# Softmax division moved behind P·V, a quarter of the transposed copies on VectorE, and a Newton root for the layer norm

## The reference

```python
# layer 0: attention with 16 heads of 32, no dependence between graphs
q = split_heads(x @ Wq.T); k = split_heads(x @ Wk.T); v = split_heads(x @ Wv.T)
bias = (adj + adj)[:, None]
a = einsum('bhnd,bhmd->bhnm', q, k) * D**-0.5 + bias
a = where(any(a != 0, axis=-1, keepdims=True), a, -inf)
p = where(isnan(softmax(a)), 0, softmax(a))
o = einsum('bhnm,bhmd->bhnd', p, v)           # -> (b, n, 512)
x = layernorm(x + o @ Wo.T)                   # (x - mean) / sqrt(var + 1e-5)
# layer 1: one of four experts per graph, batch norm over the graphs of an expert
top1 = argmax(x.mean(axis=1) @ router_w + router_b)
out = adj @ (x @ expert_w[top1])
y = relu(batchnorm_of_the_expert(out) * gamma[top1] + beta[top1])
x = layernorm(x + y)
```

## Time and profile before

| | us |
|---|---|
| median of three runs | 2745.92 |
| lowest, highest run | 2745.65, 2753.64 |
| span of the profiled execution | 2748.4 |
| of it: before the first unit's transposes | 0 to 89 |
| graph 0 | 89 to 239 |
| graphs 1 to 14, about 152 each | 239 to 2355 |
| graph 15 | 2355 to 2497 |
| tail of layer 1 | 2497 to 2580 |
| batch norm and last phase | 2580 to 2748 |

### The profile page before, as it was taken

The page is one execution under the profiler, slowest core; times in us unless marked ns, Lnnn a source line. Parts: engine busy times, 40 slices in busy tenths (PEclk is TensorE's granted clock), DMA queues, the critical chain, the costliest instruction groups (busy, mean ns, idle before and its releaser), DMA issues.

```text
span 2748.4 us, 57103 instructions
## 1 busy us (share of the span) xinstructions
PE 2333.9 (85%) x14976; PEld 1816.4 (66%) x14976; DVE 2121.6 (77%) x5107; ACT 1722.6 (63%) x3838; POOL 1771.9 (64%) x3148
## 2 busy tenths in 40 slices
PE   2778999989899898989998998989899998986533
PEld 2556777767677676767676776767677776765432
DVE  2687878788887878788887878787888878773488
ACT  0566776667666666667676666667677666763232
POOL 0777776768777777768676777767687777771000
PEclk7789998999999999999999999999999999988765
DMA  6676564645555564646455554646455555533497
GB/s 212 197 223 214 155 204 143 208 127 172 154 183 158 168 182 151 197 144 197 137 173 154 175 167 149 196 142 210 133 161 164 177 155 176 159 92 120 170 327 255
DMA packets 215956, 479.61 MB, mean 175 GB/s; under 512 B 41424, under 2 KB 49616, under 8 KB 208720
## 3 DMA queue, kind: packets, MB, share of 16 engines
q1 hardware_dynamic: 215632, 475.71, 55.1%
HBM read 274.23 MB, written 67.11 MB: 124 GB/s over the span
## 4 chain that ended last, share of the span: by engine, by line
PE 61%; DVE 17%; issue 9%; POOL 4%; ACT 3%; SPq 3%; DMA 2%; DVEq 1%; ACTq 0%; POOLq 0%
PE t_bank L334 12%; PE p_bank L252 11%; PE p_bank L253 10%; PE p_bank L254 10%; PE o_bank L347 8%; PE s_bank L325 6%; DVE att L494 3%; DVE att L468 3%; SPq L646 2%; POOL fold L617 2%; PE p_bank L288 2%; DVE ln_raw L1004 2%; POOL fold L619 1%; PE p_bank L293 1%; ACT att L407 1%
## 5 line engine op out<-in xcount | busy, mean ns | idle before, releaser
L617 POOL TENSOR_TENSOR fold<-att 128x256 f32<-128x256 f32 x1024 | 809.8, 791 | 538.7 <-DVE nmax L468 440.4
L446 ACT ACTIVATE pt<-t_bank 128x512 f32<-128x512 f32 x1024 | 610.5, 596 | 583.1 <-PE t_bank L334 571.4
L468 DVE CUSTOM_DVE_ANT_0 att<-s_bank,adj_t 128x512 f32<-128x512 f32 x1024 | 699.6, 683 | 333.9 <-PE s_bank L325 323.1
L407 ACT ACTIVATE att<-att,nmax 128x512 f32<-128x512 f32 x1024 | 737.3, 720 | 128.2 <-POOL fold L617 98.4
L494 DVE TENSOR_SCALAR att<-att,small 128x512 f32<-128x512 f32 x1024 | 739.9, 723 | 9.3
L334 PE MATMUL t_bank<-ident,att 128*128 128x128 f32 x4096 | 645.5, 282 | 46.6 <-issue 40.7
L334 PEld LDWEIGHTS t_bank<-ident,att 128*128 128x128 f32 x4096 | 515.2, 145 | 229.2 <-issue 101.8
L325 PE MATMUL s_bank<-k_stack,q_stack 128*128 128x512 f32 x1024 | 507.5, 496 | 108.0 <-DVE nmax L468 106.9
L619 POOL TENSOR_TENSOR fold<-fold 128x128 f32<-128x128 f32 x1024 | 528.2, 516 | 80.3
L624 POOL TENSOR_TENSOR fold<-fold 128x64 f32<-128x64 f32 x1024 | 351.7, 343 | 98.1 <-POOL fold L619 22.9
L347 PE MATMUL o_bank<-pt,v 128*32 128x256 f32 x4096 | 276.6, 415 | 31.9 <-ACT pt L446 15.1
(11 more groups left out here) (150 smaller groups left out, 3554.6 us busy)
## 6 DMA issues: line engine op xcount, KB each, us to landing
q_stack<-qk_t SPq DMA_DIRECT2D x1024, 64.0 KB, 2.0
k_stack<-qk_t SPq DMA_DIRECT2D x1024, 64.0 KB, 2.0
qk_w<-qk_split SPq DMA_DIRECT2D x123, 512.0 KB, 4.1
slot_a<-vo_split SPq DMA_DIRECT2D x16, 2048.0 KB, 8.0
slot_b<-vo_split SPq DMA_DIRECT2D x16, 2048.0 KB, 9.9
slot_a<-expert_split SPq DMA_DIRECT2D x16, 2048.0 KB, 7.9
stage<-in_xT SPq DMA_DIRECT2D x16, 1024.0 KB, 14.0
adj_t<-in_adj SPq DMA_DIRECT2D x64, 256.0 KB, 3.0
```

Of the source, the lines that this page charges most:

```text
L407: eng.activation(att[:, u % 4, j, :], att[:, u % 4, j, :], ACT.Exp, bias=nmax[:, u % 4, j:j + 1], scale=-1.0, accum_out=rsum[:, u % 4, j:j ...
L446: eng.activation(pt[:, j, :, (u % 2) * P:(u % 2 + 1) * P], t_bank[r % 2][:, :].rearrange("p (m n) -> p m n", m=NT), ACT.Copy).then_inc(act ...
L468: eng.tensor_tensor_reduce(out=att[:, u % 4, j, :], in0=s_bank[r % 2][:, :], in1=adj_t[:, t, :], scale=-2.0, scalar=3.0e38, op0=ALU.add, o ...
L617: eng.tensor_tensor(fold1[:, :], a[:, 0:256], a[:, 256:512], ALU.add).then_inc(pool_fold1, 1)
```

## The change

The scaling of att goes. Transposes now wait for exp alone, and ACT copies heads 0 to 2 into pt while DVE copies head 3 (DVE_TURNED, dve_turned, dve_pt). Once per pair DVE forms weight = live / rsum, 128 x 8 numbers (dve_weights, in step 3 of the pair's first unit). In pe_pv eight fp32 matmuls with the weight, broadcast to 32 columns, as stationary side and the identity as moving side write these numbers as rows into the free half of the same o_bank; P·V itself is moved from the end of the pair's second slot behind the scores of the next slot's first step, in front of that step's transposes. When the bank is emptied, ACT copies the broadcast half to spread (act_spread_out), DVE multiplies it with the product (dve_scale), and the high and low parts of ot are taken from spread. EMPTIED is later by a unit for pairs 4 to 6.

The root of the layer norm of layer 0 is computed on DVE by 13 dependent instructions on 128 x 4 numbers (dve_rstd, in (6, 2)): a first guess from the bits and three Newton steps. The square root on ACT and the reciprocal go. The statistics of M- are aggregated at once (bn_stats, bn_aggr, and one copy per graph), and the batch norm's sums take four instructions fewer. The last phase's root stays on ACT.

```diff
-NORM_UNITS = 2
+TOTAL_UNITS = 2
+DVE_TURNED = 3
...
-        EMPTIED = {0: -1, 5: 0, 7: 1, 8: 2, 9: 3, 10: 4, 12: 5, 14: 6}
+        EMPTIED = {0: -1, 5: 0, 7: 1, 8: 2, 9: 3, 11: 4, 13: 5, 15: 6}
...
+        def wait_turned(eng, b, r):
+            u, j = divmod(r, HG)
+            if j == DVE_TURNED:
+                wait(eng, dve_pt, b, UNITS, u + 1)
+            else:
+                wait(eng, act_pt, b, (HG - 1) * UNITS, (HG - 1) * u + j + 1 - (j > DVE_TURNED))
...
         def pe_turn(eng, b, r):
-            wait(eng, dve_norm, b, STEPS, r + 1)
-            wait(eng, act_pt, b, STEPS, r - 1)
+            wait(eng, act_exp, b, STEPS, r + 1)
+            wait_turned(eng, b, r - 2)
...
-        def pe_pv(eng, b, u):
-            pair, g = u // 2, u // NT
-            wait(eng, act_pt, b, STEPS, 4 * u + 4)
-            wait(eng, dve_ot, b, PAIRS, pair - 1)
-            wait(eng, act_v, b, NT, NT)
+        def pe_pv(eng, b, pair):
+            g, bank = (pair % PAIRS) // 2, o_bank[pair % 2]
+            wait(eng, dve_scaled, b, PAIRS, pair - 1)
+            wait(eng, dve_weight, b, PAIRS, pair + 1)
+            for half in range(2):
+                for j in range(HG):
+                    eng.matmul(bank[j * HD:(j + 1) * HD, (2 + half) * P:(3 + half) * P],
+                               weight[:, pair % 2, half, j:j + 1].to_broadcast([P, HD]), ident[:, :],
+                               start=True, stop=True, tile_position=(0, j * HD))
+            wait(eng, act_pt, b, (HG - 1) * UNITS, (HG - 1) * 2 * (pair + 1))
+            wait(eng, dve_pt, b, UNITS, 2 * (pair + 1))
+            if pair >= 0:
+                wait(eng, act_v, b, NT, NT)
...
+                closes = j == 0 and u >= 0 and u % 2 == 0 and (attends if u else has_prev)
+                turns = attends and r >= 0
+                if turns and not closes:
                     pe_turn(eng, b, r)
                 if (attends and r + LEAD < STEPS) or (has_next and r + LEAD >= STEPS):
                     pe_scores(eng, b, r + LEAD)
+                if closes:
+                    pe_pv(eng, b, u // 2 - 1)
+                if turns and closes:
+                    pe_turn(eng, b, r)
...
-            if attends and u >= 0 and u % 2 == 1:
-                pe_pv(eng, b, u)
...
+        def act_spread_out(eng, b, pair):
+            wait(eng, pe["pv"], b, PAIRS, pair + 1)
+            wait(eng, dve_ot, b, PAIRS, pair)
+            eng.activation(spread[:, :], o_bank[pair % 2][:, 2 * P:4 * P], ACT.Copy).then_inc(act_spread, 1)
...
-                if u == 6 and j == 3 and has_prev:
-                    wait(eng, dve_ln, b, 8, 0)
-                    eng.activation(ln_std[:, :], ln_mv[:, :, 1], ACT.Sqrt, bias=eps_c[:, :]).then_inc(act_std, 1)
...
+        def dve_turned(eng, b, r):
+            u, j = divmod(r, HG)
+            wait(eng, pe["turn"], b, STEPS, r + 1)
+            wait(eng, pe["pv"], b, PAIRS, u // 2)
+            eng.tensor_copy(pt[:, j, :, (u % 2) * P:(u % 2 + 1) * P],
+                            t_bank[r % 2][:, :].rearrange("p (m n) -> p m n", m=NT)).then_inc(dve_pt, 1)
...
-        def dve_normalise(eng, b, r):
-            u, j = divmod(r, HG)
-            eng.tensor_scalar(att[:, u % 4, j, :], att[:, u % 4, j, :], rinv[:, j:j + 1], live[:, j:j + 1],
-                              ALU.mult, ALU.mult).then_inc(dve_norm, 1)
...
+            eng.reciprocal(rinv[:, :, :], rsum[:, at, :]).then_inc(dve_stat, 1)
+            eng.tensor_tensor(weight[:, pair % 2, :, :], rinv[:, :, :], live[:, :, :],
+                              ALU.mult).then_inc(dve_weight, 1)
+        def dve_scale(eng, b, pair):
+            wait(eng, act_spread, b, PAIRS, pair + 1)
+            eng.tensor_tensor(spread[:, :], o_bank[pair % 2][:, 0:256], spread[:, :], ALU.mult).then_inc(dve_scaled, 1)
+        def dve_rstd(eng, b):
+            n = 13
...
+            link(eng.tensor_scalar(ln_var, ln_mv[:, :, 1], EPS, None, ALU.add))
+            link(eng.tensor_scalar(ln_half.bitcast(I32), ln_var.bitcast(I32), 1, None, ALU.logical_shift_right))
+            link(eng.tensor_copy(ln_std, ln_half.bitcast(I32)))
+            link(eng.tensor_scalar(ln_rstd.bitcast(I32), ln_std, -1.0, float(0x5f3759df), ALU.mult, ALU.add))
+            for _ in range(3):
+                link(eng.scalar_tensor_tensor(out=ln_half, in0=ln_var, scalar=-0.5, in1=ln_rstd, op0=ALU.mult,
+                                              op1=ALU.mult))
+                link(eng.tensor_tensor(ln_half, ln_half, ln_rstd, ALU.mult))
+                link(eng.scalar_tensor_tensor(out=ln_rstd, in0=ln_half, scalar=1.5, in1=ln_rstd, op0=ALU.add,
+                                              op1=ALU.mult))
...
+                if attends and r >= 0 and j == DVE_TURNED:
+                    dve_turned(eng, b, r)
...
+                if j == 3 and u >= 0 and u % 2 == 0 and attends:
+                    dve_weights(eng, b, u // 2)
+                if u in EMPTIED and (attends if u else has_prev):
+                    pair = EMPTIED[u]
+                    if j == 1:
+                        dve_scale(eng, b, pair)
...
+                if (u, j) == (6, 2) and has_prev:
+                    dve_rstd(eng, b)
```

More of the change, by code:

```diff
@@ L64, in build_gnn_layers @@
     PAIRS = UNITS // 2
+    BN_OPS = 2 * DT + 1
     HALF_SCALE = 0.5 * float(D) ** -0.5
@@ L114, in build_gnn_layers @@
         rb, iota4 = small[:, 4:8], small[:, 8:12]
-        total, live, rinv = small[:, 12:16], small[:, 16:20], small[:, 20:24]
         ln_std, ln_rstd = small[:, 24:28], small[:, 28:32]
         xmean = small[:, 32:36]
+        ln_var, ln_half = small[:, 12:16], small[:, 16:20]
         rt = small[:, 40:56].rearrange("p (a e) -> p a e", a=4)
@@ L122, in build_gnn_layers @@
         rsum = sb("rsum", [P, 4, HG])
+        total = sb("total", [P, 4, HG])
+        live = sb("live", [P, 2, HG])
+        rinv = sb("rinv", [P, 2, HG])
+        weight = sb("weight", [P, 2, 2, HG])
+        spread = sb("spread", [P, 2 * P])
         ln_raw = sb("ln_raw", [P, NT, 6])
@@ L417, in act_ot_hi @@
                 wait(eng, pe["O"], b, NT, 0)
-            eng.activation(ot[:, 0, g, half * 256:half * 256 + 256], o_bank[pair % 2][:, 0:256],
-                           ACT.Copy).then_inc(act_ot, 1)
+            eng.activation(ot[:, 0, g, half * 256:half * 256 + 256], spread[:, :], ACT.Copy).then_inc(act_ot, 1)
         def act_slot(eng, b, u, kind, kind_before):
@@ L441, in act_slot @@
                 r = HG * u + j
-                if attends and r >= 0:
+                if attends and r >= 0 and j != DVE_TURNED:
                     wait(eng, pe["turn"], b, STEPS, r + 1)
@@ L476, in dve_total @@
-            eng.tensor_reduce(total[:, :], fold2[:, u % 2, :, :], AX.X, ALU.add).then_inc(dve_stat, 1)
-        def dve_live(eng, b, u):
-            wait(eng, dve_norm, b, STEPS, HG * u)
-            wait(eng, dve_logit, b, STEPS, HG * (u + 1))
-            wait(eng, dve_stat, b, 3 * UNITS, 3 * u + 1)
-            eng.scalar_tensor_tensor(out=live[:, :], in0=total[:, :], scalar=0.0, in1=nmax[:, u % 4, :],
-                                     op0=ALU.not_equal, op1=ALU.logical_or).then_inc(dve_stat, 1)
@@ L486, in dve_reciprocal @@
[L486 to L495 removed]
+            eng.tensor_reduce(total[:, u % 4, :], fold2[:, u % 2, :, :], AX.X, ALU.add).then_inc(dve_total_done, 1)
@@ new lines, in dve_weights @@
+        def dve_weights(eng, b, pair):
+            at = slice(2 * pair % 4, 2 * pair % 4 + 2)
+            wait(eng, dve_total_done, b, UNITS, 2 * pair + 2)
+            wait(eng, dve_logit, b, STEPS, 2 * HG * (pair + 1))
+            wait(eng, act_exp, b, STEPS, 2 * HG * (pair + 1))
+            eng.scalar_tensor_tensor(out=live[:, :, :], in0=total[:, at, :], scalar=0.0, in1=nmax[:, at, :],
+                                     op0=ALU.not_equal, op1=ALU.logical_or).then_inc(dve_stat, 1)
+            eng.reciprocal(rinv[:, :, :], rsum[:, at, :]).then_inc(dve_stat, 1)
+            wait(eng, dve_stat, b, 2 * PAIRS, 2 * (pair + 1))
+            wait(eng, pe["pv"], b, PAIRS, pair - 1)
+            eng.tensor_tensor(weight[:, pair % 2, :, :], rinv[:, :, :], live[:, :, :],
+                              ALU.mult).then_inc(dve_weight, 1)
@@ L565, in dve_slot @@
             for j in range(HG):
-                if j == 2 and u in EMPTIED and (attends if u else has_prev):
-                    pair = EMPTIED[u]
-                    g, half = divmod(pair % PAIRS, 2)
-                    wait(eng, act_ot, b, PAIRS, pair + 1)
-                    dve_low(eng, ot[:, 1, g, half * 256:half * 256 + 256], o_bank[pair % 2][:, 0:256],
-                            ot[:, 0, g, half * 256:half * 256 + 256]).then_inc(dve_ot, 1)
                 if u == 6 and has_next:
```

90 lines of the change are left out of this document (44 added, 46 removed).

## The result

The changed kernel takes 2778.55 us (median of 4 runs, 2777.78 to 2779.87) against 2746.18 for the kernel before in the same comparison: ratio 1.0111, 95% interval 1.0097 to 1.0125. It is slower by 1.1%. The forecast was 2769, slower by 0.8%, with 2725 to 2805 as its range. The profiled execution spans 2776.6 us, 28.2 more than before.

A forecast was written before the change was run, and what follows sets the result against it. PE's in-order queue was taken as the bound: 2748.4 + 42 (14 middle iterations at +3.0) - 22 (first) + 1 (last) + 2 (tail) = 2771 us profiled, so 2769 as median; range 2725 to 2805.

The forecast's parts named there:

- Rival 4: Rival on the pair's eight matmuls: weight loads not hidden behind 128 columns, 0.9 us each time, 2813 us; chance 0.15.
- (4,0): Unit 4, step 0, a pair's closing: matmuls +0.48 us, plus +0.2 as P·V waits for DVE's copy of step 3.
- (10,0): Unit 10, step 0, a pair's closing: matmuls paid and P·V waiting for DVE's copy, +0.68 us.
- (2,0): Unit 2, step 0, a pair's closing: score and matmuls replace the 0.7 us wait for V, later score saved, -0.2 us.
- Unit 6: PE's long wait for xt in a middle iteration: removed scalings paid back by the root's 13 instructions, -0.3 us.
- Rival 2: Rival: the root's small instructions overlap, the xt wait opens, middle iterations cost nothing extra, 2729 us; chance 0.17.
- S-0 and the mean: PE's waits in a middle iteration: S-0's low part earlier, -0.6 us; router's mean behind DVE's copy and low part, +0.45.
- (0,0): Unit 0, step 0, a pair's closing in a middle iteration: the eight matmuls paid in full, +0.48 us.
- The first iteration: Graph 0: DVE relieved, POOL's folds next at 1.8 us per step, 128 us, so -22 us.
- the last iteration: Last graph: fewer chunks, second half waits for ACT's copies, a quarter fewer, against the same matmuls: +1 us.
- the tail: From 2497 us on: no attention covers layer norm, mean and router, and the root is longer on DVE: +2 us.
- one of my own signs of being wrong: Listed: middle iteration of 152 us or less, P·V waiting over 1 us for DVE's copy, or first iteration unchanged.

## Why the prediction was right, and where it was not

**The bound.** Right. PE's queue sets the time, and DVE, ACT and POOL lose 620 us of busy time together without any gain. What DVE's work still does is decide when four or five things are ready.

**The eight matmuls.** The price of eight is as forecast at both clocks, 0.46 and 0.85 us against 0.48 and 0.91. Rival 4, 0.9 each, is out: the trace has 0.46 for sixteen loads with 128 columns each. The rule of the Trainium skill that went its way (TensorE: Matmul & The Clock Gate, section "The mechanism"), by which weight loads overlap matmuls in flight only when the row group differs, is not borne out by this trace. My sum of 3.4 us per iteration for all eight pairs, less what they replace, compares with 2.9 that come back without them. That the two are near is in part luck: nothing came back ahead of the P·V of (4,0) and (10,0), where I had them paid. At (2,0) the step holds exactly when iterations of equal clock are compared: 16.66 us from V to P·V before, 16.75 after, forecast +0.1. At (10,0) P·V waits 0.5 for the copy, where I had 0.2.

**Unit 6.** Right by its mechanism: what the change frees is paid back by the root, forecast -0.3, measured +0.1. PE's wait for a logit falls by 2.3 us per iteration and that for xt grows by 2.2. That the 3 us freed come from the scalings is argued, not shown. The root is 3.37 us and not 2.7: one of the thirteen, the shift on integers, takes 0.72 against 0.17 for its neighbours, and without it my 0.21 each is met (twelve in 2.6 us). Rival 2 is right in one half: unit 6 does open, by 3 us, once the thirteen are out, and the kernel is then at 2723, near the 2729 of that rival (2727 if the 2.5 us between profile and median are taken off, as in my other sums). The thirteen do not overlap, so it did not happen.

**S-0 and the mean.** PE's wait for sup fell by 0.6 and that for the mean rose by 0.7, against -0.6 and +0.45. But the wait for x1t rose from 1.0 to 1.3 in the mean, which I had not looked at.

**The loop's turn.** Missed. I counted the matmuls of (0,0) as +0.48 and P·V's move as nothing. It is -1.2 at the turn and -0.8 behind it, by the clock that no longer falls: with the +0.1 that I had there, 2.6 us mis-sized twelve times, 31 us, partly made up by terms that came out dearer (x1t, and 0.2 here and there). The earlier trace rows had the 3.1 us of "issue" in front of PE, and the diff showed that P·V would no longer end the body; I put the two beside each other nowhere.

**The first iteration.** Missed by 16 us. I assumed POOL's folds at 1.8 us per step as next in line and let the splits' holds vanish with DVE's other work. They don't. PE's waits for a logit from 88 to 240 us, before and after:

```profile
PE s_bank L325 <- DVE nmax L468: 22.7, 14, 4.1
```

```profile
PE s_bank L333 <- DVE nmax L501: 20.4, 13, 3.8
```

POOL stands 15.5 us for DVE in four pieces, up to 8.1 us, where it stood 15.2 before. That these waits are the splits' holds is my reading; the run that was to take them away moved the loads as well.

**Graph 1, the last iteration and the tail.** Graph 1 is +7.9 where I had +3: it stands outside the loop, so has no turn to gain from, and its unit 6 was 1.9 us shorter before than that of the loop's iterations. The last iteration with the tail is +11 where I had +3. Two terms: the tail, 4.6 us against 2 (put alone into the kernel before, the Newton root adds 2.8 there and P·V moved adds 0.9), and the last iteration itself, where I gave +1 for fewer copies on ACT and it is +6.6: 2.8 ahead of sum- (the matmuls, and the root where unit 6 had been short), the rest in its second half, where PE's queue has so little else that each P·V's broadcast and its copy on DVE show (the last two pairs 1.2 and 1.6 us longer; 0.0 and 0.4 with all copies on ScalarE).

**The sum** was right for the wrong mix: the first iteration 16 us, graph 1 with the ends 13 too low, the loop 22 too high. That it came within 10 us is luck; the first iteration nearly unchanged was one of my own signs of being wrong. What I did not price at all is the copy on DVE as such. By the run that takes it back it costs 48 us, some 8 of them at the turn, more than the eight matmuls. I priced its 0.65 us as hidden, except at one P·V, since DVE is not the bound; but DVE's queue has a thing due for PE in units 4, 6, 7, 8, 9 and at the turn, and each of them was 0.2 to 0.75 us later.

The parts, from the runs, are not a sum, since each was taken alone: P·V moved 10 to 12 us faster in the kernel before and 40 in the changed one; the matmuls 32 slower; the root 45 to 55 slower; the copy on DVE 48 slower; with root and copy left as they were the change is 28 us faster than the kernel before.

## What to carry to other kernels

An engine busy for 60% is not free, as DVE shows here: each instruction put on it is paid if anything behind it in its queue is what another engine waits for. So ask of every added instruction what is due behind it, and put short dependent chains on the engine that has nothing due, even at the cost of a table load. Look at where a loop turns: in this kernel work at the end of the body on the bound engine cost more than its time, clock included, and the same work behind the next independent score cost less. When a step is moved, follow what its end triggers, loads above all.

## What was not expected of the hardware

- The turn of a loop costs PE 2.9 to 4.6 us of idle time in the kernel before, 1.5 to 2.5 in the changed one, and two stops, 1.4 to 2.3 and 2.4 to 5.5 us, with 64 more matmuls per body. It is named "issue". Behind stops of about 3 us and more in the kernel before the clock fell, at 1.5 us each, in seven of the twelve iterations counted; behind the shorter ones of the changed kernel in none.
- DVE has a stop of 3 to 5 us at the turn as well, in none of the iterations of the kernel before, in six of the changed kernel's, and it can stand ahead of the first logit (hidden) or behind it (2 us per iteration). Two kernels with the same body had it at different places.
- A shift on 128 x 4 integers took 0.72 us on DVE, the same shape in f32 0.16 to 0.17. A copy of 128 x 512 out of PSUM took 0.69, as an addition does.
- Sixteen matmul instructions of 128 fp32 columns in four strips of 32 rows take 0.46 us, a quarter of the P·V beside them, with their weight loads (PEld) recorded beside them and not between them.
